# First attention: the matmuls behind the softmax maximum contract over 64 rows instead of 128, the two heads of a pair on opposite halves of the array, head by head

## What is computed

```python
x = L0_attn_x                                  # 1 x 2048 x 128
x = x + attn1(layernorm(x))                    # 16 heads of 64, positions added to the keys, softmax over 2048 keys
x = x + ffn(layernorm(x))                      # second attention (16 heads of 8), then 4 experts by a router, two layer norms

# attn1, the part that the change touches
scores = jnp.einsum('bqhd,bkhd->bhqk', q, k) / scale
attn = jax.nn.softmax(scores, axis=-1)
out = jnp.einsum('bhqk,bkhd->bqhd', attn, v)
```

## Time and profile before

| | before |
|---|---|
| median of 3 runs | 2706.89 us (2706.29 to 2707.69) |
| profiled execution, first to last instruction | 2706.8 us |
| TensorE busy | 2573.3 us, 95% |
| DVE busy | 2049.9 us, 76% |
| ACT busy | 1106.3 us, 41% |
| POOL busy | 851.5 us, 31% |

### The profile page before, as it was taken

The page is one execution under the profiler, slowest core; times in us unless marked ns, Lnnn a source line. Parts: engine busy times, 40 slices in busy tenths (PEclk is TensorE's granted clock), DMA queues, the critical chain, the costliest instruction groups (busy, mean ns, idle before and its releaser), DMA issues. The chain is left out here.

```text
span 2706.8 us, 39054 instructions
## 1 busy us (share of the span) xinstructions
PE 2573.3 (95%) x11918; PEld 1447.8 (53%) x11918; DVE 2049.9 (76%) x3471; ACT 1106.3 (41%) x1150; POOL 851.5 (31%) x405
## 2 busy tenths in 40 slices
PE   4999999999999999999999969999999999999796
PEld 2555555555555565555555544455455445455465
DVE  6767777676767767677776779988888888898834
ACT  0333333333333333343333311556556555665332
POOL 3463645646554645636465520000000000000000
PEclk8999999999999999999999976999999999999898
DMA  4120211211211201102112110000000000000000
GB/s 113 36 52 12 48 41 25 47 29 28 55 29 34 54 13 42 46 13 48 41 24 54 34 36 5 9 7 5 7 10 5 6 5 11 5 5 8 20 0 16
DMA packets 54408, 73.00 MB, mean 27 GB/s; under 512 B 12968, under 2 KB 23872, under 8 KB 54080
## 3 DMA queue, kind: packets, MB, share of 16 engines
q1 hardware_dynamic: 54208, 70.46, 11.1%
HBM read 9.33 MB, written 1.05 MB: 4 GB/s over the span
## 5 line engine op out<-in xcount | busy, mean ns | idle before, releaser
L993 DVE TENSOR_REDUCE mxp<-ring 128x1 f32<-128x512 f32 x1640 | 1068.3, 685 | 341.3 <-PE ring L348 292.4
L655 ACT ACTIVATE prob<-scores 128x1024 f32<-128x1024 f32 x512 | 524.0, 1025 | 902.1 <-PE scores L393 877.4
L676 ACT ACTIVATE prob<-scores 128x1024 f32<-128x1024 f32 x512 | 496.8, 1022 | 414.5 <-PE scores L511 414.3
L740 POOL TENSOR_TENSOR accp<-accp,prob 128x1024 f32<-128x1024 f32 x256 | 598.1, 2370 | 0.0
L400 PE MATMUL acc_o<-prob,v 128*64 128x512 f32 x2048 | 506.3, 616 | 0.0
L353 PE MATMUL ring<-ka,kb 128*128 128x512 f32 x1104 | 448.7, 450 | 9.9 <-DVE accs L1109 3.6
L392 PE MATMUL scores<-qa,ka 128*128 128x512 f32 x1028 | 425.7, 414 | 4.6 <-issue 3.1
L348 PE MATMUL ring<-ka,qa 128*128 128x512 f32 x1064 | 417.1, 436 | 11.9 <-DMA kb<-stage_k 7.9
L393 PE MATMUL scores<-qb,kb 65*128 65x512 f32 x1028 | 407.4, 396 | 0.0
L993 DVE TENSOR_REDUCE accs<-ring 128x1 f32<-128x512 f32 x528 | 343.5, 686 | 50.6 <-PE ring L353 49.7
L353 PEld LDWEIGHTS ring<-ka,kb 128*128 128x128 f32 x1104 | 213.7, 195 | 312.9 <-DVE mxp L993 132.7
(11 more groups left out here) (105 smaller groups left out, 1366.1 us busy)
## 6 DMA issues: line engine op xcount, KB each, us to landing
ka<-stage_k SPq DMA_DIRECT2D x144, 128.0 KB, 2.3
qa<-stage_q SPq DMA_DIRECT2D x136, 128.0 KB, 2.3
kb<-stage_k SPq DMA_DIRECT2D x72, 128.0 KB, 2.3
qb<-stage_q SPq DMA_DIRECT2D x68, 128.0 KB, 2.3
kb<-stage_q SPq DMA_DIRECT2D x72, 64.0 KB, 2.0
w_sb<-w_pairs SPq DMA_DIRECT2D x10, 192.0 KB, 2.4
kb<-m_rows SPq DMA_DIRECT2D x68, 2.0 KB
qb<-m_rows SPq DMA_DIRECT2D x66, 2.0 KB
```

What stands on the lines that cost most here:

```text
L655: nc.scalar.activation(prob[:, h, j % 4, :, :], sc[h][:, :, :], ACT.Exp, scale=SCALE1).then_inc(exp_done[h], 1)
L676: nc.scalar.activation(prob[:, u, t % 4, :, :], sc[u][:, :, :], ACT.Exp, scale=SCALE2).then_inc(exp2_done[u], 1)
L740: nc.gpsimd.tensor_tensor(accp[:, h], accp[:, h], prob[:, h, j % 4], ALU.add).then_inc(pool_acc[h], 1)
L993: nc.vector.reduce_max(partial[:, h * QT + q, k:k + 1], bank[:], AX.X).then_inc(side_free, 1)
```

## The change

Four edits, all in the first attention:

- `max_tile1` contracts over 64 rows only: head 0 uses partitions 0 to 63, head 1 partitions 64 to 127. It computes (rounded query) by (rounded key); the rest of the key is left out of the maximum. The scores themselves are as before.
- So that the rounded keys of head 1 lie on partitions 64 to 127, `move_k` swaps the two halves of `ka` for head 1. The number and the size of the DMAs stay.
- `TILES1` and the start's list go through the heads innermost: head 0 and head 1 of the same queries and keys follow each other.
- TensorE's side items of a step are cut into two parts instead of three; nothing stands behind `values1` any more.

```diff
-TILES1 = [(h, q, k) for h in range(2) for q in range(QT) for k in range(NC)]
+TILES1 = [(h, q, k) for q in range(QT) for k in range(NC) for h in range(2)]
...
-    tiles = [[("max", h, q, k) for h in range(2) for q in range(QT)] for k in range(NC)]
+    tiles = [[("max", h, q, k) for q in range(QT) for h in range(2)] for k in range(NC)]
...
             def max_tile1(par, c, h, q, k):
                 bank = side()
-                nc.tensor.matmul(bank[:], qa[:, c, h, q * 128:(q + 1) * 128], ka[:, par, h, k * CW:(k + 1) * CW],
+                half = slice(64 * h, 64 * h + 64)
+                nc.tensor.matmul(bank[:], qa[half, c, h, q * 128:(q + 1) * 128], ka[half, par, h, k * CW:(k + 1) * CW],
                                  start=True, stop=True).then_inc(side_full, 1)
...
-                        parts = share(on_pe(items), 3)
+                        parts = share(on_pe(items), 2)
...
                         values1(G, par, j, 0)
                         values1(G, par, j, 1).then_inc(pv_done, 1)
-                        for it in parts[2]:
-                            item1(it, p, par, c, k, G)
...
                 for h in range(2):
                     half = slice(64 * h, 64 * h + 64)
-                    sp.dma_start(ka[0:64, par, h, cols].bitcast(F32), stage_k[half, 0, :].bitcast(F32)).then_inc(k_dma, 16)
-                    sp.dma_start(ka[64:128, par, h, cols].bitcast(F32), stage_k[half, 1, :].bitcast(F32)).then_inc(k_dma, 16)
+                    for part in range(2):
+                        at = 64 * ((h + part) % 2)
+                        sp.dma_start(ka[at:at + 64, par, h, cols].bitcast(F32), stage_k[half, part, :].bitcast(F32)).then_inc(k_dma, 16)
                     sp.dma_start(kb[0:64, par, h, cols].bitcast(F32), stage_k[half, 0, :].bitcast(F32)).then_inc(k_dma, 16)
```

## The result

The changed kernel takes 2794.16 us (2790.69 to 2798.71) against 2707.29 us: ratio 1.0323, 95% interval 1.0308 to 1.0338. It is slower by 87 us, where the forecast had 20 and its range ended at 2785. The profiled execution is 2792.4 us long.

What follows compares the result with a forecast made beforehand. TensorE was taken to bound plain steps. Saving 3.6 against price 5.0 us a chunk, less overlap and absorbed waits, gave +0.6, 20 us in 32 chunks: 2706.8 + 20 = 2727 us, range 2655 to 2785.

Steps and rivals of the forecast that it cites:

- What bounds the kernel: First attention: TensorE is the bound in plain steps of 4.85 us; in two steps of a chunk it waits for DVE.
- The gain: Tiles on opposite halves overlap fully: 18.25 slots of 0.213 us instead of 32 of 0.233, saving 3.6 us a chunk.
- Rivals 2 and 3: Pairs: halves don't overlap, 2821 us, chance 0.08; or a pair's loads go one behind the other, 2764 us, chance 0.10.
- The price: Changes between 128-row and 64-row matmuls on TensorE: 25.5 more a chunk at 0.196 us, 5.0 us a chunk.
- Rival 1: A change of shape is cheaper than with y: 0.10 us, 2669 us, chance 0.20; free, 2614 us, chance 0.06.
- The plain step: First attention: three more changes of shape less the saved slots, +0.59 - 0.51 = +0.08 us a step.
- TensorE's own sum: Price less gain in the first attention, +1.4 us a chunk, less 0.1 for y's overlap: +1.3.
- The waits: Of the +1.3 us a chunk, 0.5 at fin in step 6 and 0.2 at Q are absorbed, leaving +0.6.
- DVE's lateness as a cover: Step 2, ahead of Q: DVE's 0.57 us wait could absorb 0 to 0.57 of TensorE's losses; 0.2 taken.
- my own sentence on the burst: Two tiles at once ask for two of three banks, so a late DVE is felt one tile sooner.
- Rival 4: More gaps in TensorE's stream make the clock fall at every sums item: 41 us on top, 2768 us, chance 0.10.
- Second attention and experts: The part behind the first attention, some 1097 us, is untouched by the change.

Runs made afterwards that it cites:

- e2: The changed kernel with the old order of heads, so neighbouring 64-row tiles use the same half and can't overlap; 2875.15 us.
- e6: The changed kernel with 2 of the 8 matmuls of the sums item, output not the reference's; 2694.42 us.
- e5: The kernel before with the 8 one-column matmuls of the sums item issued twice; 2831.77 us.
- e14: The kernel before with 64-row tiles and the swapped halves only, old order, three parts; 2981.19 us.
- e4: The changed kernel with sums in two halves and one 64-row pair on either side of the value matmuls; 2681.49 us, ratio 0.992.
- e9: e4 with the 40 tiles of the start on 128 rows, same loop; 2679.6 us.
- e13: The same kernel as e9, run again; 2680.84 us, ratio 0.990.
- e7: e4's placement, but with tiles on 128 rows; 2705.03 us.
- e3: The changed kernel with the sums item cut in two, one half ahead of the scores of head 1, one behind; 2760.2 us.
- e15: e9 with the sums item whole, behind the scores of head 1, instead of in two halves; 2699.82 us.
- e12: e9 with the 8 sums matmuls laid singly between the scores (c = 2: in twos) instead of in two halves; 2700.63 us.

## Why the prediction was wrong

The direction and the mechanism of the stream were right; the clock, which makes up most of the difference, was left out of the sum, and the time left the range.

- *What bounds the kernel*: TensorE. Right: every change in its stream in plain steps came out as time.
- *The gain*: full overlap in pairs, right: 0.235 us a pair (e2), the second start 3 ns behind. Rivals 2 and 3 fell. But a slot was put at 0.213, and a matmul more or less costs 0.235 (e2 against the changed kernel). With 18.25 slots the 0.02 between them make 0.4 us a chunk, 12 us in all, that the saving was put too high.
- *The price*: 0.196 a change from the y items, 0.19 measured, and 43.3 changes a chunk in the trace, where 43.5 were counted. Rival 1 fell. The plain step was priced at +0.08 and is +0.13; with a slot of 0.233 it comes to 3 x 0.196 - 2 x 0.233 = +0.12. So TensorE's own sum is +1.7 us a chunk and not +1.3.
- *The waits*: +1.01 is left of it (32 us instead of 20, inside the bounds of 7 to 42), so about 0.7 were absorbed, as forecast, but not where I had put them. fin comes at the pace of the array, 223.46 - 223.03 = 0.43, of which nothing is a wait, where the earlier trace rows had 0.93. Over all chunks, though, fin's start was 0.58 behind the matmul before it in the mean, so no more than 0.35 was a wait, and I took 0.5. Step 7 gave some of the rest: 5.11 us before and 5.03 now, in the mean at full clock, while a plain step got 0.13 longer. In step 2, where I had DVE's lateness as a cover, nearly nothing was absorbed (6.24 before, 6.32 now); the wait ahead of Q is now one inside a pair, as my own sentence on the burst said. These are the rows of the changed kernel for fin (L361) and for step 2, where a pair takes 0.97 us instead of 0.50 since its second tile waits 0.48 for a bank:

```profile
223.03 0.50 PE L349 MATMUL ring<-ka,qa 64*128 64x512 f32 x1
223.46 0.27 PE L361 MATMUL ring<-ident,mx 128*8 128x128 f32 x1
...
739.30 0.97 PE L349 MATMUL ring<-ka,qa 64*128 64x512 f32 x2
740.20 0.50 PE L393 MATMUL scores<-qa,ka 128*128 128x512 f32 x1
```

- *The clock*: this is the step that failed. Rival 4 had the right place (the sums item), nearly the right size (41 us; it is 51), the wrong reason and the wrong standing. Its reason was more gaps in TensorE's stream; there are fewer, busy 1406.36 of 1410 us after and 1396.00 before, and the clock falls all the same. As for its chance, I read "rare" off and gave 0.10, though the earlier trace rows shows the clock falling in a stretch in which TensorE is busy for all of its time. The busy share says nothing of how much of the array works; the change halves the rows of 32 tiles a chunk and adds 25 changes of shape, and I didn't ask what that does to a clock that already falls on small matmuls. And as for its form, it isn't an alternative to the forecast but comes on top of it, and so on top of the stream's own 32 us. 2707 + 32 + 51 = 2790 is made of terms that both stood in the text, each within the bounds given there; the profile's other 3 us are the start's.
- *Second attention and experts*: unchanged, right.

Of the Trainium skill, "TensorEngine Tiling (Array Packing)", Key Properties, says that changing the tiling mode drains TensorE; the runs agree that a change costs time (0.19 us here). Of the Trainium skill, "TensorE: Matmul & The Clock Gate", Part 3, has packed matmuls start 4 ns apart; the trace has 3. The section on HAM oscillation of the same page of the Trainium skill warns of idle gaps between matmuls; the three stretches of e6 stand behind such gaps, but in the changed kernel the clock fell with none, PE busy 43.40 of the 43.40 us before the fall and 3.40 of 3.40 us in it.

## What to carry to other kernels

Before packing matmuls on opposite halves, count the changes of shape, not the halves: a pair of 512-column matmuls saves 0.235 us and a way in and out costs 0.39 (two changes), so a single pair among full-height matmuls loses, and one next to work of yet another shape (where a way is paid anyway) wins: 0.6 us a chunk here. Read the granted clock around the emptiest item of TensorE's stream before thinning out its neighbours, and add that term to the forecast instead of setting it beside it. And look for the extra wait in the steps with the dear items, not in the plain ones.

## What the runs showed of the hardware

- Two matmuls on opposite row halves start 3 ns apart and take the time of one: what follows starts 0.43 us behind the pair (729.34 to 729.77), as behind a single 64-row tile (223.03 to 223.46).
- A change between 128-row and 64-row matmuls costs 0.19 to 0.20 us: 0.09 to 0.10 at the change and 0.10 for the first load of weights, in both directions, for float32 (y) and float32r (tiles) alike. Changes between 128 and 65 rows cost nothing (starts 0.23 to 0.24 apart).
- The granted clock fell to its lower level with TensorE's queue full, by one-column matmuls alone (e5: 31 stretches with 3.6 us of them a chunk, against 7 with 1.8), and in the start it stayed down for longer with 64-row matmuls instead of 128-row ones (a mean of 0.50 to 0.53 against 0.59 to 0.69 at the same pace, with no one-column matmul).
- In the loop the two act together: 64-row tiles with most of the one-column matmuls gone leave 3 stretches (e6), 64-row tiles with all of them in one piece 26 to 28 (changed, e2, e14). 64-row tiles beside the value matmuls, with the sums in halves, have no more than 128-row tiles in the same places (e4, e9, e13: 27 to 51 us; e7: 48 us).
- Cutting 1.8 us of one-column matmuls into halves brought 34 us (e3) and 19 us (e15 against e13), cutting them into eighths nothing (e12). I can't say why.
